# Spline stage: half the norms and both weight splits on GpSimd, both bounds in one series of halvings; local attention: first splits ahead of the scatters

## The reference, cut to what matters

```
# L0_ffn, on xf = layernorm with gamma, beta, of the normalised x
best_cluster = argmax(sign(xf) @ cluster_sigs.T)
tile_idx = argmax(where(in_cluster, sign(xf) @ tile_sigs.T, -inf))     # one of 64 tiles of 4 features per token
x_slice = the 4 features of the token's tile
tile_min = min over all tokens of a tile of x_slice.min;  tile_max likewise
u = clip((x_slice - tile_min) / (tile_max - tile_min + 1e-8), 0, 1 - 1e-6)
delta = spline of u (16 cells, base + slope) * output_scale
x = x + (layernorm of x + delta placed at the 4 features)
# L1_attn: x = x + window_attention(layernorm(x)), 16 heads of 16, windows of 64
```

## Time and profile before

| | us |
|---|---|
| median of 3 runs (1044.77 to 1046.61) | 1045.63 |
| the profiled execution | 1046.12 |
| its span, first to last instruction | 1044.3 |
| TensorE busy in the span | 987.1 (95%) |
| VectorE busy | 772.3 (74%) |
| ScalarE busy | 701.9 (67%) |
| GpSimd busy | 330.7 (32%) |

### The profile page before, as it was taken

One profiled execution on the slowest core, in us unless ns is written; L12 is line 12 of the kernel. 1 busy time (PEld: TensorE's weight loads), 2 busy tenths in 40 slices (PEclk: granted clock), 3 DMA queues, 4 the chain that ended last, 5 costly groups with the idle time before them and its releaser, 6 DMA issues. The chain is left out here.

```text
span 1044.3 us, 19330 instructions
## 1 busy us (share of the span) xinstructions
PE 987.1 (95%) x6896; PEld 818.3 (78%) x6925; DVE 772.3 (74%) x1525; ACT 701.9 (67%) x1959; POOL 330.7 (32%) x276
## 2 busy tenths in 40 slices
PE   7999999999999999999999988699999989899997
PEld 3898888888998899889988866577777789774444
DVE  5798867667676676776757989899998644567774
ACT  5888876777767776776662358487788535448882
POOL 1343333322333233323310120054545310106672
PEclk9999999999999999999999998999999999899999
DMA  7322000000000001000205000000000000018652
GB/s 211 94 61 61 1 2 1 2 1 1 2 1 1 1 2 36 2 1 1 82 16 132 1 1 1 1 2 2 1 2 2 2 1 2 8 51 277 217 180 81
DMA packets 31841, 40.21 MB, mean 39 GB/s; under 512 B 8193, under 2 KB 23297, under 8 KB 31745
## 3 DMA queue, kind: packets, MB, share of 16 engines
q1 hardware_dynamic: 31744, 38.98, 11.9%
HBM read 36.74 MB, written 2.23 MB: 37 GB/s over the span
## 5 line engine op out<-in xcount | busy, mean ns | idle before, releaser
L349 POOL TENSOR_TENSOR roped_q<-roped_q,sin_q 128x512 f32<-128x512 f32 x64 | 82.0, 1281 | 302.3 <-DVE sin_q L494 302.3
L1664 ACT ACTIVATE win_P<-banks,win_neg_max 128x128 f32<-128x128 f32 x256 | 91.4, 382 | 27.6 <-DVE win_neg_max L1740 27.3
L349 POOL TENSOR_TENSOR roped_k<-roped_k,sin_k 128x512 f32<-128x512 f32 x64 | 83.2, 1301 | 46.6 <-DVE sin_k L494 46.6
L403 ACT ACTIVATE P<-banks,neg_max 128x128 f32<-128x128 f32 x256 | 90.5, 372 | 6.9 <-DVE neg_max L519 6.6
L437 ACT ACTIVATE oT_hi<-banks,bv_col 128x512 fp32r<-128x512 f32 x64 | 44.1, 690 | 74.2 <-PE banks L667 74.2
L1601 POOL TENSOR_TENSOR win_P<-win_P,win_inv 128x512 f32<-128x512 f32 x64 | 66.9, 1046 | 70.4 <-DVE win_inv L1745 70.3
L412 ACT ACTIVATE sin_k<-banks 64x512 f32<-64x512 f32 x128 | 76.0, 594 | 11.6 <-PE banks L37 10.1
L522 DVE SCALAR_TENSOR_TENSOR oT_lo<-banks,bv_col,oT_hi 128x512 fp32r<-128x512 f32 x64 | 47.9, 749 | 42.6 <-ACT oT_hi L437 42.0
L412 ACT ACTIVATE sin_q<-banks 64x512 f32<-64x512 f32 x128 | 76.0, 594 | 2.9 <-PE banks L37 0.7
L629 PE MATMUL banks<-WO_lo,oT_hi 128*128 128x256 f32 x256 | 72.9, 285 | 0.0
L493 DVE SCALAR_TENSOR_TENSOR roped_k<-banks,qk_bias,cos 128x512 f32<-128x512 f32 x64 | 48.0, 750 | 33.2 <-ACT sin_k L412 33.2
(11 more groups left out here) (428 smaller groups left out, 3141.2 us busy)
## 6 DMA issues: line engine op xcount, KB each, us to landing
ret_V<-moe_gate_rows SPq DMA_DIRECT2D x16, 512.0 KB, 4.8
ctx<-moe_gate_rows SPq DMA_DIRECT2D x16, 512.0 KB, 5.2
X<-in_x SPq DMA_DIRECT2D x4, 512.0 KB, 6.6
stage<-in_wqT SPq DMA_DIRECT2D x4, 512.0 KB, 4.1
stage<-in_wvT SPq DMA_DIRECT2D x4, 512.0 KB, 5.9
stage<-in_woT SPq DMA_DIRECT2D x4, 512.0 KB, 4.3
ctx<-in_ctxT SPq DMA_DIRECT2D x4, 512.0 KB, 5.8
out<-X SPq DMA_DIRECT2D x8, 256.0 KB, 2.4
```

The source lines that it names most:

```text
L349: nc.gpsimd.tensor_tensor(roped[w][:, p, :], roped[w][:, p, :], sin_part[w][:], ALU.add).then_inc(roped_sum[w], 1)
L403: ins = nc.scalar.activation(P[:, i, :], SC[:, i * 128:(i + 1) * 128], ACT.Exp, bias=neg_max[:, r % 2, i:i + 1], accum_out=exp_sum[:, r % ...
L1664: ins = nc.scalar.activation(P[:, h % 2, s, i, :], SC[2 * (h % 2) + s][:, i * 128:(i + 1) * 128], ACT.Exp, bias=neg_max[:, h % 2, at:at + ...
```

## The change

In the spline block:

- Groups 2 and 3 are normalised by GpSimd, group 2 from the start of the block, group 3 behind the late statistics. VectorE's list loses these eight instructions.
- GpSimd makes `win_qk_lo` and `win_w_lo`, each as soon as ScalarE has rounded its weight.
- The high value is reduced with `negate=True`, so that both bounds are minima: one addition of 128x2048 and one series of halvings over both replace the two. `place_high` goes. Both transposes wait for one semaphore.
- TensorE scores groups 1 and 2 and transposes `hot` of the first half before it transposes and scores group 3; ScalarE's list follows.

In the window block `split_q` and `split_k` of pair 0 come before batch 4, batches 5 to 15 go to other ticks, part 1 to tick 2, and pair 2 is normalised in tick 3 instead of 2.

```diff
 # phase_spline, GpSimd
+                normalise(2)            # tensor_scalar of 128x256, four batches, then_inc(xn_pool, 1)
                 pool.wait_ge(stat, 8)
                 nc.gpsimd.tensor_tensor(rstd12[:, LATE], var12[:, LATE], minus_half[:, LATE], ALU.pow).then_inc(rstd12_ready, 1)
+                pool.wait_ge(rstd12_ready, 1)
+                normalise(3)
                 nc.gpsimd.tensor_tensor(rstd[:, LATE], var_eps[:, LATE], minus_half[:, LATE], ALU.pow).then_inc(rstd_ready, 1)
+                pool.wait_ge(win_rounded, 1)
+                nc.gpsimd.tensor_tensor(kept["win_qk_lo"][:], w["win_wqk"][:], kept["win_qk_hi"][:].bitcast(F32), ALU.subtract).then_inc(win_split, 1)
+                pool.wait_ge(win_rounded, 2)
+                nc.gpsimd.tensor_tensor(kept["win_w_lo"][:], w["win_w_in"][:], kept["win_w_hi"][:].bitcast(F32), ALU.subtract).then_inc(win_split, 1)
 # phase_spline, ScalarE
                 take_signs(2)
+                take_hot(0)
+                take_hot(1)
                 take_signs(3)
...
-                for b in range(B):
-                    place_high(b)
 # phase_spline, VectorE
-                normalise(2)
-                dve.wait_ge(rstd12_ready, 1)
-                dve.wait_ge(stat, n)
-                normalise(3)
...
-                reduce(lo_hi[:, 1, :], xs[:], AX.X, ALU.max).then_inc(high_known, 1)
+                reduce(lo_hi[:, 1, :], xs[:], AX.X, ALU.max, negate=True)
                 link(reduce(lo_hi[:, 0, :], xs[:], AX.X, ALU.min))
                 dve.wait_ge(off_ready, 2)
-                link(TT(extreme[:, 0], off[:], over(lo_hi[:, 0, :], NT), ALU.add))
-                extreme_of(0, ALU.min)
-                dve.wait_ge(win_rounded, 1)
-                TT(kept["win_qk_lo"][:], ...)
-                dve.wait_ge(high_placed, B)
-                extreme_of(1, ALU.max)
+                link(TT(extreme[:], off[:] (twice), lo_hi[:] (over the 64 tiles), ALU.add))
+                for m in (8, 4, 2):
+                    link(TT(extreme[:, :, 0:m], extreme[:, :, 0:m], extreme[:, :, m:2 * m], ALU.min))
+                TT(tile_ext[:], extreme[:, :, 0], extreme[:, :, 1], ALU.min).then_inc(ext_ready, 1)
...
-                dve.wait_ge(win_rounded, 2)
-                TT(kept["win_w_lo"][:], ...)
 # phase_spline, TensorE, after score_tiles(0)
-                for g in range(1, NG):
-                    if g + 1 < NG:
-                        transpose_x(g + 1)
-                    score_tiles(g)
+                transpose_x(2)
+                score_tiles(1)
+                score_tiles(2)
+                transpose_hot(0)
+                transpose_hot(1)
+                transpose_x(3)
+                score_tiles(3)
 # phase_window, VectorE
+        FINISHED = 5, 6, 7, None, 8, 9, 10, 11, None, 12, None, 13, None, 14, None, 15      # batch of each tick
                 finish_part(0)
+                split_q(0)
+                normalise(1)
+                split_k(0)
                 finish_batch(4)
-                normalise(1)
-                finish_batch(5)
-                split_q(0)
-                finish_batch(6)
-                split_k(0)
...
-                    if p == 2 and m + 2 < PAIRS + CROSS:
+                    if p == (2 if m > 0 else 3) and m + 2 < PAIRS + CROSS:
                         normalise(m + 2)
```

More of the change, by code:

```diff
@@ L1214, in _, with pool_link, normalise @@
             def _(pool):
+                count = [0]
+                def pool_link(ins):
+                    count[0] += 1
+                    ins.then_inc(pool_chain, 1)
+                    pool.wait_ge(pool_chain, count[0])
+                def normalise(g):
+                    for b in range(GROUP * g, GROUP * (g + 1)):
+                        nc.gpsimd.tensor_scalar(XN[:, b, :], X[:, b, :], mean[:, b:b + 1], rstd12[:, b:b + 1], ALU.subtract, ALU.mult).then_inc(xn_pool, 1)
+                normalise(2)
                 pool.wait_ge(stat, 8)
                 nc.gpsimd.tensor_tensor(rstd12[:, LATE], var12[:, LATE], minus_half[:, LATE], ALU.pow).then_inc(rstd12_ready, 1)
+                pool.wait_ge(rstd12_ready, 1)
+                normalise(3)
                 nc.gpsimd.tensor_tensor(rstd[:, LATE], var_eps[:, LATE], minus_half[:, LATE], ALU.pow).then_inc(rstd_ready, 1)
+                pool.wait_ge(win_rounded, 1)
+                nc.gpsimd.tensor_tensor(kept["win_qk_lo"][:], w["win_wqk"][:], kept["win_qk_hi"][:].bitcast(F32), ALU.subtract).then_inc(win_split, 1)
+                pool.wait_ge(win_rounded, 2)
+                nc.gpsimd.tensor_tensor(kept["win_w_lo"][:], w["win_w_in"][:], kept["win_w_hi"][:].bitcast(F32), ALU.subtract).then_inc(win_split, 1)
                 pool.wait_ge(next_stat, 2 + 7)
@@ L1266, in _ @@
                 for i in range(2):
-                    for g in (2 * i, 2 * i + 1):
-                        take_hot(g)
+                    if i == 1:
+                        take_hot(2)
+                        take_hot(3)
                     make_off(i)
@@ L1427, in transpose_x @@
                 def transpose_x(g):
-                    pe.wait_ge(xn_ready, GROUP * (g + 1))
+                    if g < 2:
+                        pe.wait_ge(xn_ready, GROUP * (g + 1))
+                    else:
+                        pe.wait_ge(xn_pool, GROUP * (g - 1))
                     wait(pe, signs_ready, KD * (g - 1))
@@ L1480, in _ @@
                 score_tiles(0)
-                for g in range(1, NG):
-                    if g + 1 < NG:
-                        transpose_x(g + 1)
-                    score_tiles(g)
+                transpose_x(2)
[5 more added lines that the diff above has]
+                score_tiles(3)
                 for i in range(2):
-                    for g in (2 * i, 2 * i + 1):
-                        transpose_hot(g)
+                    if i == 1:
+                        transpose_hot(2)
+                        transpose_hot(3)
                     for p in range(4 * i, 4 * i + 4):
@@ L1592, in power @@
                     return nc.gpsimd.tensor_tensor(rstd[:, some], var_eps[:, some], minus_half[:, some], ALU.pow)
-                for part in range(2):
-                    pool.wait_ge(stat, stat_done[part])
-                    power(PARTS[part]).then_inc(rstd_ready, 1)
+                pool.wait_ge(stat, stat_done[0])
+                power(PARTS[0]).then_inc(rstd_ready, 1)
                 for h in range(TICKS):
```

42 lines of the change are left out of this document (17 added, 25 removed).

## The result

| | before | after |
|---|---|---|
| median, us | 1046.12 (14 runs, 1043.33 to 1049.86) | 1050.05 (14 runs, 1046.48 to 1052.85) |
| profiled execution, its span | 1046.12, 1044.3 | 1051.85, 1050.1 |

The ratio is 1.0036 with a 95% interval from 1.0022 to 1.0051: the change makes the kernel slower by 2.3 to 5.3 us.

The account below looks back on a forecast made before the run. VectorE's list was taken as the path in the spline block and window front. Spline +2.05 and window -0.3 gave +1.75 on 1046.12, so 1047.9, or 1047.4 as the median lies 0.5 lower; range 1042.6 to 1050.8.

Parts of the forecast that it names:

- the rival of slow norms: Spline block: GpSimd's TENSOR_SCALAR takes 1.0 us or more, group 3's norms reach the choice and gather; 1050.7; chance 0.19.
- group 3: Spline block: GpSimd's norms from about 620.9 to 623.1 may meet one VectorE TENSOR_SCALAR; +0.1 us (0 to 0.3).
- the first split: Spline block, second choice: GpSimd's split holds until about 632 and VectorE's TENSOR_SCALAR waits; +0.7 us (0.2 to 1.6).
- Price of a GpSimd TENSOR_SCALAR: Norms on GpSimd, 128x256: 0.55 us each, between the cast's 0.45 and the TENSOR_TENSOR's 0.78.
- The norms of group 2 against VectorE's: Start of spline block: GpSimd's norms delay VectorE's four by 0.9, less 0.40 gained; net +0.5 us (-0.4 to +1.4).
- Series: Spline block, first addition to sum of look-ups: one series for both bounds, 8.29 to 7.34; -0.95 us (-1.3 to -0.6).
- Second split: Spline block: GpSimd holds to 641.9, VectorE's addition at 640.19 waits; +1.7 us (1.3 to 2.2).
- The sign that the prediction named: 128x2048 addition in the spline block: if it stays at 2.29, the split costs nothing and the prediction is 1.7 too high.
- TensorE's new order: Spline block: group 3's scores come before the second choice; first-half look-ups end later but aren't needed for 8 us; no cost.
- Window: Window front to ninth maxima: first maxima 2.4 us earlier, but the lead mostly isn't kept; -0.3 (-2.3 to +1.2).

Follow-up runs that it names:

- the probe: Kernel before plus sixteen 128x256 GpSimd operations into a scratch tile, four forms: norm's form 1.27 us, one operation 0.93, constants 1.09, copy 0.41.

## Why the prediction was right and where it was wrong

It said slightly slower, 1047.4 in a range of 1042.6 to 1050.8, and the time is 1050.05: inside the range, near its upper end, with the sign right. That it is inside is partly luck: the block moved by 5.34 where the sum had 2.05, more than all its upper bounds together (4.9), and the range reached so far only for the rival of slow norms. Of the 3.3 too little, 2.15 is group 3 and 1.33 the first split. Term by term:

- **Price of a GpSimd TENSOR_SCALAR: wrong, and the cause of most of the miss.** Taken at 0.55 between bounds of 0.45 (the cast) and 0.78 (the TENSOR_TENSOR); measured 1.22 to 1.28. Both bounds came from other forms, and the reason given for the lower one, one input, doesn't hold: the probe has a copy at 0.41 and the two-operation form at three times that. The Trainium skill, GPSIMD Engine Reference, section "Engine selection", puts one-input work on GpSimd roughly at line rate. The copy agrees (0.41, where VectorE's addition of this size takes 0.42 in the earlier trace rows), the TENSOR_SCALARs (0.93 to 1.27) don't, and the measurement decides.
- **The norms of group 2 against VectorE's: +0.5 predicted, +0.23 measured at the choice; the hold was wrong.** VectorE's first four went from 1.37 to 1.52, not to 2.2, although GpSimd's ran beside them throughout; three of group 1's, which the sum left out, went from 1.05 to 1.43. A TENSOR_SCALAR of GpSimd stretches VectorE's, but doesn't hold them for its length as its TENSOR_TENSOR does.
- **Group 3: +0.1 predicted, +2.25 measured.** The step that failed is "Group 3 follows the late power, from about 620.9 to 623.1". At 1.22 each it ended at 626.4, and the second power, which the next instruction of VectorE behind the choice needs, stood behind it in the queue. I had asked whom the norms would meet and not what was queued behind them. The rival of slow norms named the price (1.0 or more), had group 3's norms end at about 627, and came within 0.7 of the time (1050.7), but by another way: it had the norms stretch VectorE's instructions.
- **First split: +0.7 predicted, +2.03 measured**, above the bound of 1.6. VectorE was about 2 behind the forecast by then, so the split met the halvings and not the second choice. The mechanism (one holder, the other waits) was right, the collision another.
- **Series: -0.95 predicted, -0.76 measured**, inside the bounds; with the splits timed 7.35 instead of the forecast 7.34. But all of it is the splits' leaving; the series itself is worth nothing (+0.13).
- **Second split: +1.7 predicted, +1.6 measured**, at a small product ahead of the addition. What counts is the split's length less what VectorE still does beside it. The sign that the prediction named misled: the addition kept its 2.29, and the split was not free.
- **TensorE's new order: nothing predicted, nothing measured in the changed kernel.** But the prediction asked only about the look-ups of the first half; those of the second came 0.27 to 1.45 late in the four kernels of this order where the second split didn't cover it.
- **Window: -0.3 predicted.** The first maxima came 2.26 early, as forecast (2.4). The ninth came +2.13 in the changed kernel's profile and -0.46 to +2.17 in the other kernels with this order and no fillers, and the medians show no loss. The forecast that the lead isn't kept held; its size can't be told finer than that.

What stays open: the block alone says +5.3, the medians +3.9 (2.3 to 5.3). Every kernel with a measured median lies about 0.5 to 2.7 us under what its block alone would give. The intervals are as wide as this difference. Part of it goes with the granted clock, as a mean over a whole execution. In 31 of 80 executions of before, run beside the experiments, it was 0.979 or less, with a median time of 1048.96 against 1045.79 in the others. The series alone, which has before's window order, shows the same in 5 of 12, and the five kernels with the new window order and VectorE's norms in none of 57. So the new order's small gain in the medians goes with fewer executions at a low clock. Among executions at 0.984 or more, the kernels that give GpSimd nothing new, or only the timed splits, lie within 0.6 of what their block says against before's. The changed kernel and those of its variants that have such executions still lie 1.1 to 2.3 under. This is a reading of the runs afterwards, with few executions on some sides; no run changes the clock alone, and the rest of the difference has no cause here.

## What to carry to other kernels

Before work goes to an idle engine, price the exact form of instruction there, and then look at what stands behind it in that engine's queue: a free engine that serves short, urgent steps has a queue like any other. In this kernel a GpSimd TENSOR_TENSOR cost VectorE most of its length where VectorE works from SBUF and nothing where VectorE reads PSUM or reduces, so its place matters more than its price: cut into pieces and released by VectorE's own progress, the same splits cost 0 instead of 3.6 us.

## What was not expected of the hardware

- GpSimd's TENSOR_SCALAR of 128x256 with two operations and per-row scalars takes 1.22 to 1.32 us, three times its copy of the same size (0.41) and 1.6 times its TENSOR_TENSOR (0.78 in the earlier trace rows).
- It stretches VectorE's TENSOR_SCALARs by a tenth to a third (1.37 to 1.52 for four, 1.05 to 1.43 for the next three), while a GpSimd TENSOR_TENSOR stops one (0.20 to 2.15). In the other direction VectorE's 128x2048 product stretched four such GpSimd norms from 4.87 to 6.66.
- Which of the two engines waits goes by who starts first, by less than 0.1: at 641.35 against 641.44 GpSimd waited 2.1 and VectorE's following halving 2.0, and 643.05 against 643.14 in another kernel gave the same.
- TensorE's pauses of 1.59 and 1.54 us were followed by a granted clock of 0.57 over 8 us, in which eight matmuls took 3.78 instead of 1.99.
